# Attention on one Trainium2 core: the product with the values taken per 128 queries of both halves, one block of four key chunks per tile

## What is computed

```
op = argmax(h[0, 0, :19])
q, k, v = h @ wq[op], h @ wk[op], h @ wv[op]
attn = softmax(einsum('bqd,bkd->bqk', q, k) / 8)
y = einsum('bqk,bkd->bqd', attn, v) @ wo[op]
h = where(am[op], y, h)
z = relu(h @ w1[op] + b1[op]) @ w2[op] + b2[op]
h = where(fm[op], z, h)
```

## Time and profile before

| what | us |
|---|---|
| median of 3 runs | 298.6 |
| lowest and highest run | 296.65, 299.23 |
| the profiled execution, its own time | 296.85 |
| its span (first to last instruction) | 295.1 |
| mean granted TensorE clock | 0.93 of full |
| PE, DVE, ACT busy | 242.3, 204.4, 176.0 |

### The profile page before, as it was taken

The page is one execution under the profiler, slowest core; times in us unless marked ns, Lnnn a source line. Parts: engine busy times, 40 slices in busy tenths (PEclk is TensorE's granted clock), DMA queues, the critical chain, the costliest instruction groups (busy, mean ns, idle before and its releaser), DMA issues.

```text
span 295.1 us, 4926 instructions
## 1 busy us (share of the span) xinstructions
PE 242.3 (82%) x1530; PEld 150.8 (51%) x1531; DVE 204.4 (69%) x360; ACT 176.0 (60%) x327; POOL 57.5 (19%) x80
## 2 busy tenths in 40 slices
PE   7889946999999820686679699999999999968950
PEld 3344825787777420432166466665656556535410
DVE  1377787778777456488657987788697686617793
ACT  2619212575667754384428986788777688615741
POOL 9600042454530033002300000002000200210131
PEclk9999985999999975599779999999999999997997
DMA  7920000000000000000000000000000000000033
GB/s 170 191 45 1 3 0 0 1 2 0 0 0 0 28 0 6 3 2 9 13 17 0 0 2 0 0 2 0 2 0 0 2 0 2 0 0 2 0 71 72
DMA packets 3304, 4.78 MB, mean 16 GB/s; under 512 B 1042, under 2 KB 2258, under 8 KB 3283
## 3 DMA queue, kind: packets, MB, share of 16 engines
q1 hardware_dynamic: 2758, 3.86, 6.0%
q10 hardware_dynamic: 524, 0.64, 0.8%
HBM read 3.45 MB, written 1.05 MB: 15 GB/s over the span
## 4 chain that ended last, share of the span: by engine, by line
PE 66%; DVE 14%; issue 10%; ACT 5%; POOL 1%; DVEq 1%; ACTq 0%; POOLq 0%
PE ps L573 11%; PE ps L603 11%; PE ps L585 10%; PE ps L439 6%; PE ps L471 4%; PE ps L460 4%; PE ps L673 3%; DVE arena L999 3%; DVE h_st L1084 3%; PE ps L416 2%; PE ps L450 2%; PE ps L378 2%; PE ps L662 2%; PE ps L353 2%; ACT sq L894 2%
## 5 line engine op out<-in xcount | busy, mean ns | idle before, releaser
L325 POOL TENSOR_TENSOR tabs<-x,h 128x512 f32<-128x512 f32 x16 | 22.7, 1418 | 179.7 <-DVE h L1146 112.5
L1129 DVE TENSOR_REDUCE negmax<-ps 128x1 f32<-128x1024 f32 x32 | 39.1, 1224 | 21.9 <-PE ps L573 21.6
L877 ACT COPY arena<-ps 128x1024 f32<-128x1024 f32 x32 | 32.4, 1012 | 21.5 <-PE ps L585 21.3
L573 PE MATMUL ps<-h_st,g_st 128*128 128x512 f32 x128 | 38.9, 426 | 2.4 <-ACT pr L836 2.4
L836 ACT ACTIVATE pr<-ps,negmax 128x1024 f32<-128x1024 f32 x32 | 35.8, 1117 | 5.1 <-DVE negmax L1129 4.7
L603 PE MATMUL ps<-arena,vk 128*64 128x256 f32 x256 | 38.2, 398 | 0.5 <-ACT arena L877 0.5
L585 PE MATMUL ps<-eye,pr 128*128 128x128 f32 x256 | 34.6, 278 | 2.1 <-DVE pr L1139 1.9
L585 PEld LDWEIGHTS ps<-eye,pr 128*128 128x128 f32 x256 | 27.9, 141 | 13.2 <-DVE pr L1139 6.7
L755 ACT ACTIVATE prob<-ps,negmax 128x308 f32<-128x308 f32 x32 | 16.3, 513 | 29.2 <-DVE negmax L1010 29.2
L662 PE MATMUL ps<-h_st,w_st 128*128 128x512 f32 x64 | 20.4, 465 | 14.6 <-ACT w_st L886 9.9
L573 PEld LDWEIGHTS ps<-h_st,g_st 128*128 128x128 f32 x128 | 21.9, 188 | 16.6 <-issue 9.9
(11 more groups left out here) (110 smaller groups left out, 375.0 us busy)
## 6 DMA issues: line engine op xcount, KB each, us to landing
arena<-in_key_onehot SPq DMA_DIRECT2D x4, 361.0 KB, 6.2
out<-tabs SPq DMA_DIRECT2D x8, 128.0 KB, 2.3
x<-in_x SPq DMA_DIRECT2D x2, 256.0 KB, 5.7
x<-in_x ACTq DMA_DIRECT2D x2, 256.0 KB, 5.6
w1d<-in_ffn_w SPq DMA_DIRECT2D x4, 64.0 KB, 2.1
w2p<-in_ffn_pack SPq DMA_DIRECT2D x2, 65.5 KB, 1.9
spread_w<-in_spread_mat SPq DMA_DIRECT2D x4, 32.0 KB, 5.7
mean_w<-in_mean_mat SPq DMA_DIRECT2D x1, 96.0 KB, 2.2
```

What stands on the lines that cost most here:

```text
L325: nc.gpsimd.tensor_tensor(osum[:, s], x2f[:, s], h2[:, s], ALU.add).then_inc(S["summed"], 1)
L573: mm = nc.tensor.matmul(ps[:, 2 * h + c, :], g_st[:, b2, h, q0:q0 + P], h_st[:, b2, h, part, c * 512:c * 512 + 512], start=(part == 0), st ...
L877: nc.scalar.copy(prt[:, n // 8 % 2, n % 2, :, q0:q0 + P], ps[:, 4:6, :].rearrange("p b (c q) -> p (b c) q", c=4)).then_inc(S["s_pt"], 1)
L1129: nc.vector.tensor_reduce(negmax[:, 0, n % 2:n % 2 + 1], ps[:, 2 * (n % 2):2 * (n % 2) + 2, :], mybir.AxisListType.XY, ALU.max, negate=Tru ...
```

## The change

The product with the values is cut otherwise. `mix(j, half)` takes the place of `mix_chunk`: j is 128 queries of both halves (2 tiles), and a call does 4 key chunks for both halves, 8 matmuls of 128 columns (16 records). One call stands in every tile from n = 3, between `tile_scores(n+2)` and `tile_turn(n)`; `mix(14, 1)` follows `mix(14, 0)` at n = 31, and only `mix(15, 0)` and `mix(15, 1)` stand behind the last tile. The buffers and their waits move with it. The values of pair 0 come after `tile_scores(1)` at the head. The queries of pair 1 are both in bank 6 (GBANK), later, each behind the `query_low` of the one before. The lists of extra pieces on ACT and DVE are rearranged.

```diff
-GBANK = (2, 6, 7, 6)
+GBANK = (2, 6, 6, 6)
...
-                    if (b2, c) == (1, 1):
-                        pe.wait_ge(S["g_low"], 8 * a + 4)
+                    if b2 == 1:
+                        pe.wait_ge(S["g_low"], 8 * a + 4 + 2 * c)
...
-                def mix_chunk(k, c):
+                def mix(j, half):
 
-                    g, cols = k // 2, slice(k % 2 * 256, k % 2 * 256 + 256)
-                    if c == 0:
-                        pe.wait_ge(S["s_pt"], base + 4 * k + 4)
-                        if k == 0:
-                            pe.wait_ge(S["g_low"], 8 * a + 6)
-                        if k == 2:
+                    g, cols = j // 4, slice(j % 4 * P, j % 4 * P + P)
+                    if half == 0:
+                        pe.wait_ge(S["s_pt"], base + 2 * j + 2)
+                        if j == 4:
                             pe.wait_ge(S["vo_copied"], 3 * a + 3)
-                        if k == 4:
+                        if j == 8:
                             pe.wait_ge(S["decided"], a + f + 2)
-                        if k >= 4 and k % 2 == 0:
+                        if j in (8, 12):
                             pe.wait_ge(S["a_stored"], 4 * a + g - 1)
-                    for h in range(2):
-                        mm = nc.tensor.matmul(ps[C * h:C * h + C, 7 - g % 2, cols],
-                                              vk[:, k // 4, c, C * h:C * h + C],
-                                              prt[:, g % 2, h, c, cols],
-                                              start=(c == 0), stop=(c == NKC - 1))
-                    if k % 2 == 1 and c == NKC - 1:
+                    for c in range(4 * half, 4 * half + 4):
+                        for h in range(2):
+                            mm = nc.tensor.matmul(ps[C * h:C * h + C, 7 - g % 2, cols],
+                                                  vk[:, g // 2, c, C * h:C * h + C],
+                                                  prt[:, g % 2, h, c, cols],
+                                                  start=(c == 0), stop=(c == NKC - 1))
+                    if j % 4 == 3 and half == 1:
                         mm.then_inc(S["s_pv"], 1)
...
                 queries(0, 0)
-                pe.wait_ge(S["fold_d"], a + 2)
                 pe.wait_ge(S["section_done"], a + f + 1)
-                values(0, range(NKC), 4)
                 tile_scores(0)
                 tile_scores(1)
+                pe.wait_ge(S["fold_d"], a + 2)
+                values(0, range(NKC), 4)
                 for n in range(NT):
                     if n + 2 < NT:
                         tile_scores(n + 2)
-                    if n >= 4 and n % 4 > 0:
-                        mix_chunk(n // 4 - 1, n % 4 * 2)
+                    if n >= 3:
+                        mix((n - 3) // 2, (n - 3) % 2)
+                    if n == NT - 1:
+                        mix(14, 1)
                     tile_turn(n)
                     if n == 0:
                         queries(0, 1)
-                    if n == 1:
+                    if n == 3:
                         queries(1, 0)
-                    if n == 3:
+                    if n == 5:
                         queries(1, 1)
-                    if n == 6:
+                    if n == 7:
                         pe.wait_ge(S["g_low"], 8 * a + 8)
                         values(1, range(4), 6)
-                    if n == 8:
+                    if n == 9:
                         pe.wait_ge(S["vo_copied"], 3 * a + 2)
                         values(1, range(4, NKC), 6)
-                    if n >= 4 and n % 4 == 0:
-                        mix_chunk(n // 4 - 1, 0)
-                    if n >= 4:
-                        mix_chunk(n // 4 - 1, n % 4 * 2 + 1)
-                    if n == 14:
+                    if n == 13:
 
                         pe.wait_ge(S["a_stored"], 4 * a + 1)
                         turn_row(7)
-                for c in range(NKC):
-                    mix_chunk(NT // 4 - 1, c)
+                mix(15, 0)
+                mix(15, 1)
...
                 between = {1: lambda: (query_high(0, 1, 0), query_high(0, 1, 1)),
-                           2: lambda: (query_high(1, 0, 0), query_high(1, 0, 1)),
-                           3: lambda: high(2, 0),
-                           4: lambda: (query_high(1, 1, 0), query_high(1, 1, 1)),
-                           5: lambda: high(2, 1), 7: lambda: copy_values(1, 1, 0, 6, 1),
-                           8: lambda: low(parts, 2, 0),
-                           9: lambda: (copy_values(2, 1, 4, 6, 1), low(parts, 2, 1)),
-                           10: lambda: (high(3, 0), high(3, 1)),
-                           12: lambda: low(parts, 3, 0), 13: lambda: low(parts, 3, 1),
+                           2: lambda: high(2, 0), 3: lambda: high(2, 1),
+                           4: lambda: (query_high(1, 0, 0), query_high(1, 0, 1)),
+                           6: lambda: (query_high(1, 1, 0), query_high(1, 1, 1)),
+                           7: lambda: low(parts, 2, 0),
+                           8: lambda: copy_values(1, 1, 0, 6, 1),
+                           9: lambda: low(parts, 2, 1),
+                           10: lambda: (copy_values(2, 1, 4, 6, 1), high(3, 0)),
+                           11: lambda: high(3, 1),
+                           13: lambda: low(parts, 3, 0), 14: lambda: low(parts, 3, 1),
...
-                           23: lambda: next_high(1, 0), 24: lambda: next_high(1, 1),
+                           22: lambda: next_high(1, 0), 23: lambda: next_high(1, 1),
...
                 between = {2: lambda: (query_low(0, 1, 0), query_low(0, 1, 1)),
-                           3: lambda: (query_low(1, 0, 0), query_low(1, 0, 1)),
-                           5: lambda: (query_low(1, 1, 0), query_low(1, 1, 1)),
-                           7: lambda: high_low(parts, 2, 0), 8: lambda: high_low(parts, 2, 1),
-                           11: lambda: high_low(parts, 3, 0), 12: lambda: high_low(parts, 3, 1),
-                           13: lambda: store(0), 15: lambda: decide(a + f + 1, 7, ev),
+                           4: lambda: (query_low(1, 0, 0), query_low(1, 0, 1)),
+                           5: lambda: high_low(parts, 2, 0),
+                           6: lambda: (query_low(1, 1, 0), query_low(1, 1, 1)),
+                           8: lambda: high_low(parts, 2, 1),
+                           11: lambda: store(0),
+                           12: lambda: high_low(parts, 3, 0), 13: lambda: high_low(parts, 3, 1),
+                           14: lambda: decide(a + f + 1, 7, ev),
                            17: lambda: next_high_low(0, 0), 18: lambda: next_high_low(0, 1),
-                           21: lambda: store(1),
-                           24: lambda: next_high_low(1, 0), 25: lambda: next_high_low(1, 1),
-                           29: lambda: store(2)}
+                           19: lambda: store(1),
+                           23: lambda: next_high_low(1, 0), 24: lambda: next_high_low(1, 1),
+                           27: lambda: store(2)}
```

## The result

The changed kernel takes 306.1 us (median of 4 runs, 304.29 to 308.17), the kernel before 297.79 beside it. The ratio is 1.027, with an interval of 1.021 to 1.034: slower, by 8 us. A second measurement gave 304.6, ratio 1.025 (1.018 to 1.031). The forecast was 298.9, with no change as the likeliest case; the range ended at 303.5, and the measured time lies outside it.

What follows compares the result with a forecast made beforehand. PE was taken to bound the attention; a steady gain of about 6 us and 1.2 at the end were eaten by 8.15 of waits. With the head, 0.0 or +1.55 gave a forecast of 298.9 us, range 294 to 303.5.

Steps and rivals of the forecast that it cites:

- no change as the likeliest case: Whole kernel: no change of note, 0 to +1.55 us as summed, own range 296.5 to 301; chance 0.60.
- query halves: Tiles 5 and 7: query_high and query_low of pair 1 at the same n delay the transposes, 5.15 us a step.
- (a): Before transposes of tiles 5 and 7: PE waits for pair 1's query pieces on ACT and DVE, 2.14 us each, 4.3 together.
- (b): Scores issued at tiles 14 and 15: PE waits for ACT's low pieces of pair 1's keys, 1.45 + 1.7 = 3.15 us.
- (c): Product of tile 11: mix(4, 0) waits for pair 1's values, copied on ACT behind copy(10), 0.7 us.
- DVE keeps up: Steady tiles with extra pieces: DVE just fits PE's 3.01 us; bound 0 to 0.3 for each pair, taken as 0.
- the second of the two cases: Head: clock stays at 1.2 GHz, scores take 1.73 each, transposes start 0.4 us later than before; likelier, two to one.
- the fall of the clock in the gaps: Gaps before tiles 5 and 7: low clock adds 3.0 us, giving +4.55, about 303; chance 0.15.
- dense work on both sides: Gaps before tiles 5 and 7: argument that PE's work around each gap speaks against a falling clock; no size of its own.
- ACT has 2.0 of exponentials and copy a tile, 0.62 of an extra piece, and fits: Steady tiles: ACT's busy times taken to fit within PE's 3.01 us a tile.
- the two frames: Whole kernel: profiled execution of 296.85 us and median of the runs, 298.6, 1.75 above it.

Runs made afterwards that it cites:

- e4: Changed kernel with query_high of pair 1, low(3, h) and the values of pair 1 each one tile earlier: 293.6 us, ratio 0.984 to the kernel before.
- e5: As e4, but each mix call cut in two of 8 records, one before and one behind the transposes: 299.6 us, ratio 1.009 to the kernel before.
- e1: Changed kernel with the two query_high of pair 1 one tile earlier on ACT (n = 3 and 5): 299.1 us, ratio 1.004 to the kernel before.
- e2: Changed kernel with low(3, 0) and low(3, 1) one tile earlier on ACT (n = 12 and 13): 300.6 us, ratio 1.009 to the kernel before.
- e7: As e4, with ACT's extra pieces spread to one at each n from 6 to 13: 293.6 us, ratio 0.986 to the kernel before.
- e8: As e7, with every extra piece of ACT between the exponentials and the next n's copy: 290.4 us, ratio 0.976 to the kernel before.
- e3: Changed kernel with matmuls of zeros on PE in the gaps at tiles 5, 7, 14 and 15, all waits kept: 301.1 us, ratio 1.011 to the kernel before.
- e9: Kernel before, with only ACT's extra pieces moved between the exponentials and the next n's copy: 297.5 us, ratio 0.999 to the kernel before.

## Why the prediction was wrong, point by point

The steps on the path, from the start of transposes to the next, in us. "Now" is the first profiled execution, "again" the second, "all" is e4.

| step | put | now | again | all |
|---|---|---|---|---|
| first queries to transposes 0 | 9.9 | 10.15 | 10.05 | 10.14 |
| transposes 0 to 4 | 13.1 | 13.15 | 13.15 | 13.15 |
| 4 to 5, query halves | 5.15 | 5.10 | 5.10 | 2.99 |
| 5 to 6 | 3.85 | 5.50 | 5.52 | 3.84 |
| 6 to 7, query halves | 5.15 | 5.10 | 5.10 | 2.97 |
| 7 to 8 | 3.86 | 5.42 | 3.86 | 3.87 |
| 8 to 11 | 10.6 | 10.55 | 10.55 | 10.58 |
| 11 to 13 | 6.0 | 6.24 | 6.23 | 6.23 |
| 13 to 14 | 4.65 | 5.05 | 5.06 | 3.09 |
| 14 to 15 | 4.7 | 6.49 | 5.05 | 3.13 |
| 15 to 29 | 42.1 | 42.86 | 42.75 | 42.75 |
| 29 to the last product | 9.15 | 9.34 | 9.34 | 9.34 |

**What held.** That PE bounds the attention, and that the product's entries, not its columns, are what the change saves: steady tiles of 2.97 to 2.99 where 3.01 was put, and e5 shows the entry alone. The waits (a), (b) and (c) appear at the tiles named, released by the engines named; (a) is within 0.05 us, and (c) is 0.66 idle for 0.7 put. e1 takes (a) away, e2 (b), and e7 (c). DVE keeps up, as put: in e8 the steps over its extra pieces behind tile 15 are 2.97 to 2.99. At the head the second of the two cases came, the scores at 1.2 GHz (8 in 3.78 busy), 10.15 and 10.05 where 9.9 was put. The Trainium skill says on the page "TensorEngine Tiling (Array Packing)", section "Key Properties", that "Mode switching requires drain"; the trace agrees in that an entry and the way back cost 0.35 (e5) beyond the streaming; that it is a drain, or the change of the weights' width at all, no run shows. The Trainium skill's page "TensorE: Matmul & The Clock Gate", section "Back-to-back issue gap", gives a sustained 81 ns for a matmul of 128 columns. The trace has 1.03 for 16 records of this kind, 64 ns each with the entry and all, and the measurement decides.

**What failed, first and largest: the clock.** The prediction had the fall of the clock in the gaps as a rival with a chance of 0.15, and only for the two gaps of (a). The sum needed it as a term. It is 4.8 us in the first execution (1.65 and 1.56 behind the gaps of (a), 1.5 behind the second of (b)) and 1.67 in the second, and 3.5 in the median by e3. I had in my hands that the clock fell at the head after PE's idle 2.19, and had made gaps of 2.14 myself; "dense work on both sides" was no reason to put the chance that low.

**Second: (b) was undersized.** Put 1.45 and 1.7, measured 5.06 less 3.08, and 5.05 less 3.14: 1.98 and 1.91, together 0.75 more. The term counted 1.65 from the end of the transposes, with 0.90 for the copy; ahead of a `low` the copy takes 1.04 from start to start. In the trace it is 1.82 (transposes end at 215.39 + 1.09 = 216.48, scores start at 218.30), and PE would have begun the scores 0.24 before that end, since scores follow transposes by 0.85 from start to start and not by 1.09.

**Third: "ACT has 2.0 of exponentials and copy a tile, 0.62 of an extra piece, and fits".** Busy time fits, the order doesn't: behind a piece that touches partitions 64 to 127 a chain of 4.07 stands against 3.8 of PE. It costs 0.27 in four steps after tile 15 and in one before, 1.35 us, less some 0.4 by which the other tiles beat 3.01. e8, where these steps are gone, shows it. I had looked at DVE's order in this manner and not at ACT's.

Together: 118.2 was put for the attention (116.64 and 1.55), 121.78 and 124.95 came. Of the 3.6 in the second execution 1.7 are the clock, 0.75 (b), 0.9 the steps after tile 15 and from 11 to 13 (the ACT chain), and 0.35 the head and the end. Of the 0.19 at the end, 0.09 is misread: transposes 29 to 30 took 2.29 in the kernel before, and do now, where 2.2 was put. That the forecast of 298.9 lies between the two frames added nothing to the error that matters.

One thing outside the attention: the first queries start at 146.98 in the profile of before and at 149.13 and 147.89 in the two of the changed kernel, though nothing up to there was changed. 1.27 of the 2.15 us arise at once: the 10 matmuls of zeros with which each execution begins take 6.05 before, 7.32 and 6.59 in the changed kernel. The two executions of the changed kernel start their first queries 1.24 apart, so this much comes from the execution and not from the change. Whether all of it does, one profile of each other kernel doesn't show: those that enter the product twice a tile have 146.98, 146.88 (e5) and 146.86 (e9), all the others 147.66 to 149.64.

## What to carry to other kernels

When list entries are moved in a hand-ordered pipeline, write down for each which engine's piece of the same n it waits for: a producer and a consumer at the same index, with the consumer ahead of the next tile's work, turn a hidden split into 2 us of idle for the engine that bounds everything. Price a gap on TensorE with the slow clock behind it, not with its length alone; if it can't be removed, filling it with useless matmuls is worth trying. And before trusting "it fits" by busy time, add up the chain from one engine's release to the next use: here a piece put where its engine waits anyway was free, and the same piece behind the copy was not.

## What was unexpected of the hardware

Behind a gap of the same 2.1 us the granted clock was low in one execution and full in another of the same kernel (tile 7: 5.42 with PEclk 0.70, or 3.86 with 1.00). Over the profiles of the changed kernel (two), e1 and e2 it was low behind 7 of 12 gaps: 3 of 3 before tile 5, 2 of 3 before tile 7, none of 3 at the first gap of (b) and 2 of 3 at the second. Useless matmuls in a gap made the kernel 3.5 us faster. And 16 matmul records of 128 columns with 64-wide weights take no longer than 8 of 256 (1.03 and 1.02), though they need twice as many weight loads; what costs is to enter the product and leave it again, 0.35 us each time. And on ACT a piece of 64 partitions costs 0.25 us more between its neighbours when it touches partitions 64 to 127 than on 0 to 63 alone (1.68 against 1.43).
